# A mixture-of-experts step threaded through attention: expert tiles, sorting and fetching moved to other blocks

## The chip, the cores and the metric

The kernel runs on one core of a Trainium2 chip. The metric is the device time of one execution in microseconds. TensorE is called PE, VectorE DVE, ScalarE ACT, GpSimd POOL and SyncE SP, as in the profile.

## The reference

```python
xn = _layernorm(x)                                   # x is (1, 2048, 128)
# attention: 16 heads of 64, no mask
q, k, v = (xn @ W for W in (Wq, Wk, Wv))
attn = softmax(einsum('bqhd,bkhd->bhqk', q, k) * SCALE)
att = einsum('bhqk,bkhd->bqhd', attn, v).reshape(b, s, H * DH) @ Wo + bo
# experts: each token goes to one of 8, by the largest router logit
expert = argmax(softmax(xn @ router_w.T))
h = square(relu(xn @ expert_fc[expert]))             # 128 -> 512
ffn = h @ expert_proj[expert].T                      # 512 -> 128
return x + att + ffn
```

## The kernel before

The attention is cut into 32 blocks: 8 pairs of heads by 4 column blocks of 512 queries. Block n works on pair n // 4 and queries n % 4. A block has 16 steps kt, one for each 128 keys. In each step PE makes the scores of both heads (two matmuls each, lines 969 and 973, into the banks SB), ACT turns them into exponentials (line 529, five buffers per head and a sixth for the last step), and PE makes for the next block the scores whose row maxima are needed there (line 985, banks MB, three of them), which DVE reduces (line 677). Every fourth step PE multiplies the last four steps' exponentials with V (times_v, line 997, 3.6 us). The exponentials are added up over the steps for the denominators: for head 1 always by POOL (line 430), for head 0 in turns by POOL (steps given by on_pool) and by DVE (add_own, line 693, at steps 0, 4, 8, 12, up to four of them in a row).

Around this, each block has small jobs at fixed steps, all of which pass through the one spare bank XB, whose users wait for one another: the denominators (step 4), the inversion by DVE in two halves (steps 4 and 8, line 809), the normalisation by POOL (step 9, line 436), the projection by Wo (step 11, line 1043), summed into Y by DVE (line 816), the turned row maxima (step 12), Q for the block three ahead (step 7), and K or V of the next pair (steps 1 and 9; blocks with n % 4 of 0 or 1 make K, the others V; the last four blocks make neither). SP issues the copies of Q and K, the row maxima, and all loads from its one queue, in program order.

The experts work on sorted tokens. In the prologue PE makes the router's logits, choose() takes each token's expert. In block 0, rank() (from line 766) computes for each token its slot in a list sorted by expert, padded to tiles of 128, and which expert owns each of the 23 tiles. POOL writes the 16 groups of 128 tokens to their slots in DRAM (sort_tokens, line 454, one indirect DMA each), two per step in the second half of block 0. The tokens come from xn, which lies in the buffer V[1]. In blocks 1 to 23, one tile each, SP loads the tile's tokens and its expert's weights at the block's beginning (load_tile), PE turns the tokens at step 2, multiplies up at step 3 and down at step 6, ACT and POOL do the parts between, and SP stores the result. In block 28 POOL fetches the results of all tokens, 16 indirect DMAs (fetch_results, line 460), into V[0], and in block 29 DVE adds them to Y in four parts (take_back, line 795).

All engines run their own lists in program order and wait for semaphores, so an engine that waits holds up everything behind it in its list.

## Time and profile before

| | us |
|---|---|
| median of 3 runs (1451.12 to 1452.48) | 1451.62 |
| the profiled execution | 1452.27 |
| its span | 1450.5 |
| PE busy | 1398.2 (96%) |
| DVE busy | 1162.4 (80%) |
| ACT busy | 737.3 (51%) |
| POOL busy | 1075.5 (74%) |

The profile is one execution; 1.8 us lie outside its span. Blocks are cut below at the start of the copy in line 566, which ends each block's sum with V. A busy PE can still run at half clock, so the granted clock is read beside the busy time.

### The profile page before, as it was taken

The numbers are of one execution on the slowest core, as the hardware profiler recorded it, in microseconds if no ns is written. First come the engines' busy times: TensorE is split into PE (matmuls) and PEld (weight loads), VectorE is DVE, ScalarE is ACT, GpSimd is POOL, SyncE is SP. The second block draws the span as 40 slices with busy tenths as digits, with TensorE's granted clock in tenths as the row PEclk, the third lists the DMA queues.
The fourth block names the chain that finished last, engine by engine and source line by source line (L and its number), as shares of the span: only waits on it lengthen the run. The fifth ranks groups of instructions, "written<-read, shape, count | busy, mean of one in ns | idle before, by whom it ended". The sixth has DMA issues, their size and how long they took to land.

```text
span 1450.5 us, 20040 instructions
## 1 busy us (share of the span) xinstructions
PE 1398.2 (96%) x6427; PEld 862.4 (59%) x6427; DVE 1162.4 (80%) x1550; ACT 737.3 (51%) x1314; POOL 1075.5 (74%) x851
## 2 busy tenths in 40 slices
PE   5876999999999999999999999999999999999997
PEld 3544665665666665666665666666656565655553
DVE  7875878877888877888878887887788888889865
ACT  4333554555554554554555555555555455544553
POOL 8266777777777777777776777777777777788887
PEclk9898999999999999999999999999999999999998
DMA  3422211321122311132112221122111220001000
GB/s 80 108 62 61 58 41 41 82 63 45 28 62 69 86 25 35 44 90 64 40 25 60 68 64 41 41 68 66 43 41 24 66 68 23 23 24 28 1 15 15
DMA packets 64967, 72.09 MB, mean 50 GB/s; under 512 B 8928, under 2 KB 38112, under 8 KB 64864
## 3 DMA queue, kind: packets, MB, share of 16 engines
q1 hardware_dynamic: 63840, 68.72, 19.2%
q0 software_dynamic: 1024, 2.10, 0.5%
q8 instruction: 52, 0.85, 0.3%
q14 instruction: 51, 0.42, 0.1%
HBM read 17.83 MB, written 5.11 MB: 16 GB/s over the span
## 4 chain that ended last, share of the span: by engine, by line
PE 89%; DVE 5%; POOL 3%; issue 2%; ACT 1%; DMA 1%; POOLq 0%; SPq 0%; DVEq 0%; ACTq 0%
PE OB L997 29%; PE SB L969 17%; PE MB L985 15%; PE SB L973 15%; PE XB L1034 2%; PE XB L1043 2%; PE XB L1025 2%; DVE mx L677 2%; PE XB L952 1%; PE XB L959 1%; POOL acc L430 1%; DVE acc L693 1%; POOL sorted_x L454 1%; PE XB L1004 1%; PE XB L1006 1%
## 5 line engine op out<-in xcount | busy, mean ns | idle before, releaser
L430 POOL TENSOR_TENSOR acc<-acc,ex 128x512 f32<-128x512 f32 x662 | 872.1, 1338 | 171.1 <-ACT ex L529 143.1
L529 ACT ACTIVATE ex<-SB 128x512 f32<-128x512 f32 x1024 | 608.6, 599 | 476.9 <-PE SB L973 420.1
L677 DVE TENSOR_REDUCE mx<-MB 128x1 f32<-128x512 f32 x1024 | 682.5, 686 | 200.5 <-PE MB L985 198.4
L997 PE MATMUL OB<-ex,V 128*64 128x512 f32 x2048 | 467.0, 598 | 0.0
L969 PE MATMUL SB<-Q,K 128*128 128x512 f32 x1024 | 427.9, 418 | 0.0
L985 PE MATMUL MB<-K,Q 128*128 128x512 f32 x1024 | 407.4, 402 | 15.3 <-DVE mx L677 13.9
L973 PE MATMUL SB<-Q,K 128*128 128x512 f32 x1024 | 402.5, 393 | 1.6 <-DMA Q<-mrow 1.6
L693 DVE TENSOR_TENSOR acc<-acc,ex 128x512 f32<-128x512 f32 x234 | 290.3, 1241 | 38.9 <-POOL acc L430 26.7
L997 PEld LDWEIGHTS OB<-ex,V 128*64 128x64 f32 x2048 | 138.6, 137 | 271.3 <-issue 239.7
L969 PEld LDWEIGHTS SB<-Q,K 128*128 128x128 f32 x1024 | 194.2, 190 | 139.3 <-issue 103.0
L985 PEld LDWEIGHTS MB<-K,Q 128*128 128x128 f32 x1024 | 194.9, 191 | 66.9 <-DVE mx L677 23.9
L973 PEld LDWEIGHTS SB<-Q,K 128*128 128x128 f32 x1024 | 194.0, 189 | 33.1 <-DMA Q<-mrow 2.1
L430 POOL TENSOR_TENSOR acc<-ex 128x512 f32<-128x512 f32 x63 | 79.6, 1284 | 96.3 <-ACT ex L529 96.2
L809 DVE RECIPROCAL rd<-rd 128x256 f32<-128x256 f32 x62 | 108.0, 1742 | 0.0
L436 POOL TENSOR_TENSOR osb<-osb,rd 128x512 f32<-128x512 f32 x31 | 39.7, 1281 | 85.3 <-DVE rd L809 85.3
L566 ACT ACTIVATE osb<-OB 128x512 f32<-128x512 f32 x32 | 19.1, 598 | 101.0 <-PE OB L997 101.0
L1034 PE MATMUL XB<-acc,ones 128*64 128x512 f32 x128 | 34.5, 617 | 2.7 <-POOL acc L430 2.7
L1025 PEld LDWEIGHTS XB<-wraw,xT 128*128 128x128 f32 x256 | 34.4, 195 | 2.5
L799 DVE SCALAR_TENSOR_TENSOR qlo<-XB,qhi 128x512 fp32r<-128x512 f32 x31 | 21.4, 692 | 17.8 <-ACT qhi L540 17.6
L1043 PEld LDWEIGHTS XB<-wo,osb 128*128 128x128 f32 x248 | 32.5, 191 | 3.8 <-issue 1.4
L1025 PE MATMUL XB<-wraw,xT 128*128 128x128 f32 x256 | 34.5, 279 | 0.0
L1043 PE MATMUL XB<-wo,osb 128*128 128x128 f32 x248 | 32.7, 275 | 1.0 <-issue 1.0
(126 smaller groups left out, 566.8 us busy)
## 6 DMA issues: line engine op xcount, KB each, us to landing
Q<-qhi SPq DMA_DIRECT2D x124, 128.0 KB, 2.3
K<-khi SPq DMA_DIRECT2D x112, 128.0 KB, 2.3
Q<-qlo SPq DMA_DIRECT2D x64, 128.0 KB, 2.3
K<-klo SPq DMA_DIRECT2D x56, 128.0 KB, 2.3
w<-fc SPq DMA_DIRECT2D x23, 256.0 KB, 2.7
w<-projT SPq DMA_DIRECT2D x23, 256.0 KB, 3.1
sorted_x<-res SPq DMA_DIRECT2D x1, 1472.0 KB, 7.0
tok<-sorted_x SPq DMA_DIRECT2D x23, 64.0 KB, 1.7
```

Source lines behind the costliest of these rows:

```text
L430: pool.tensor_tensor(a[:, :], src[:, :], EX[h][ex_slot(kt)][:, :], ALU.add).then_inc(done, 1)
L529: act.activation(EX[h][ex_slot(kt)][:, :], SB[in_ring(2 * kt + h)][:, :], ACT.Exp).then_inc(a_e[h], 1)
L677: dve.tensor_reduce(mx[:, m % 2, u:u + 1], MB[in_ring(i)][:, :], AX.X, ALU.max).then_inc(v_m, 1)
L693: dve.tensor_tensor(a[:, :], src[:, :], EX[0][ex_slot(kt)][:, :], ALU.add).then_inc(sums[0][n % 2], 1)
L809: dve.reciprocal(rd[:, cols], rd[:, cols]).then_inc(v_rd, 1)
L969: pe.matmul(tile[:, :], K1[par][h][:, keys], Q1[k][h][:, :], start=True, stop=False)
L973: pe.matmul(tile[:, :], K2[par][h][:, keys], Q2[k][h][:, :], start=False, stop=True).then_inc(t_s, 1)
L985: pe.matmul(MB[in_ring(i)][:, :], Q1[k][h][:, q * P:(q + 1) * P], K1[par][h][:, c * QB:(c + 1) * QB], start=True, stop=True).then_inc(t_m, 1)
L997: mm = pe.matmul(OB[own[h], :], V[(n // JB) % 2][:, k, own[h]], EX[h][ex_slot(k)][:, :], start=(k == 0), stop=(k == NT - 1))
L1025: mm = pe.matmul(XB[:, k * P:(k + 1) * P], xT[:, tok], wraw[pair % 2][:, 2, :], start=True, stop=True)
L1034: mm = pe.matmul(XB[own[h], :], ones[:, 0:DH], acc[h][n % 2][:, :], start=True, stop=True)
L1043: mm = pe.matmul(XB[:, q * P:(q + 1) * P], on[:, q * P:(q + 1) * P], wo_s[pair % 2][:, :], start=True, stop=True)
```

## The change

Tiles are worked on in blocks 3 to 25 instead of 1 to 23. SP stores a tile's result and loads the next tile in the middle of a block, behind the K copies and ahead of the Q copies; the first tile is loaded at the end of block 2. The ranking's matmuls move from step 5 to step 3 of block 0, and rank() is cut in three, for steps 4, 8 and 12; the owners of the tiles are found in block 1, step 12. The 16 sorts go one by one into steps 13 to 15 of block 0 and 1 to 13 of block 1. ACT therefore waits for them before it overwrites V[1] in block 2. The fetches go into blocks 28 and 29 (five each) and 30 (six), and their target is the buffer xT. take_back is moved to steps 1, 2, 3 and 5 of block 31, and the sums into Y that come after it wait for it. The division of head 0's additions changes: in block 0 POOL takes all steps with kt % 4 of 1 or 2, in block 1 only those with 1, and block 28, where DVE had all of them, is like the others.

```diff
--- before.py
+++ after.py
@@ -92,8 +92,13 @@
 AT_INV, AT_ON = (4, 8), 9
 AT_TOK, AT_UP, AT_DOWN = 2, 3, 6
 TILES = NT + E - 1
-AT_Q2, AT_RANK = 2, 5
-BACK = (4, 5, 6, 7)
+TILE0 = 3
+AT_Q2, AT_RANK = 2, 3
+AT_PLACE, AT_OWN = (4, 8, 12), (1, 12)
+SORT = [(0, kt) for kt in range(13, NT)] + [(1, kt) for kt in range(1, 14)]
+FETCH = [(n, kt) for n in (NB - 4, NB - 3) for kt in (2, 5, 8, 11, 14)] + [(NB - 2, kt) for kt in range(2, 13, 2)]
+BACK = (1, 2, 3, 5)
+assert FETCH[0][0] >= TILE0 + TILES and len(SORT) == len(FETCH) == NT
 
 
 def layer(nc, x, wq, wk, wv, wo, bo, router_wT, fc, projT, out):
@@ -130,6 +135,7 @@
         acc = [[sb(f"acc{h}{k}", [P, QB]) for k in range(2)] for h in range(2)]
 
         xn = V[1]
+        back = xT[:, :].rearrange("p (t d) -> p t d", d=D)
         halves, mean_var = sb("halves", [P, NT, 6]), sb("mean_var", [P, NT, 2])
         std, rstd = sb("std", [P, NT]), sb("rstd", [P, NT])
         bob, eps = sb("bob", [P, D]), sb("eps", [P, 1])
@@ -214,9 +220,7 @@
 
         def on_pool(n, kt):
 
-            if n.i is None and n.off == NB - JB:
-                return False
-            return kt % BATCH == 1 or (kt % BATCH == 2 and (n.i is not None or n.off > 0 or kt > NT - BATCH))
+            return kt % BATCH == 1 or (kt % BATCH == 2 and n.off != 1)
 
         def ex_slot(kt):
 
@@ -284,7 +288,7 @@
 
         def has_tile(n):
 
-            return n.i is not None or 0 < n.off <= TILES
+            return TILE0 <= n.off < TILE0 + TILES
 
         with nc.Block() as block:
             @block.sync
@@ -382,25 +386,27 @@
 
                 def one(n):
                     pair = n // JB
-                    if has_tile(n):
-                        sp.wait_ge(d_sort, 16 * NT)
-                        sp.wait_ge(v_own, 1)
-                        load_tile(n - 1)
                     if n % JB == 1:
                         if before(n, NB - 2 * JB):
                             load_w(pair + 2)
                     spread = kv_jobs(n) if before(n, NB - JB) and n % JB < 2 else [None, None]
                     if spread[0]:
                         spread_k(*spread[0][1:])
+                    if has_tile(n):
+                        store_tile(n - TILE0)
+                    if has_tile(n + 1) and n.off >= TILE0:
+                        load_tile(n + 1 - TILE0)
                     for kt in range(NT):
                         for m in q_jobs(n, kt):
                             spread_q(m)
                     if spread[1]:
                         spread_k(*spread[1][1:])
-                    if has_tile(n):
-                        store_tile(n - 1)
                     if n % JB == 1 and before(n, NB - JB):
                         load_wo(pair + 1)
+                    if n.off == TILE0 - 1:
+                        sp.wait_ge(d_sort, 16 * NT)
+                        sp.wait_ge(v_own, 1)
+                        load_tile(Lin(0))
                     if before(n, NB - 1):
                         place_max(n + 1)
 
@@ -408,6 +414,7 @@
                     ov = out.rearrange("o (t p) d -> p (o t) d", p=P)
                     for j in range(JB - 1):
                         sp.wait_ge(v_y, NB - JB + j + 1)
+                        sp.wait_ge(v_back, j + 1)
                         sp.dma_start(chunk(ov, j), chunk(Y, j)).then_inc(d_out, 16)
                     for q in range(TB):
                         k = NT - TB + q
@@ -455,9 +462,9 @@
 
                 def fetch_results(ks):
                     pool.wait_ge(d_res, 16 * (TILES + 1))
-                    pool.wait_ge(t_pv, NT * (NB - JB))
+                    pool.wait_ge(t_v, NB)
                     for k in ks:
-                        pool.indirect_dma_start(V[0][:, k, :], None, sorted_y, indexed(k)).then_inc(d_back, 16)
+                        pool.indirect_dma_start(back[:, k, :], None, sorted_y, indexed(k)).then_inc(d_back, 16)
 
                 def first():
                     pool.memset(res[:, :], 0.0).then_inc(g_i, 1)
@@ -506,14 +513,14 @@
                         if kt == AT_ON and not (n.i is None and n.off == 0):
                             normalise(n - 1)
                         if kt == AT_UP + 1 and has_tile(n):
-                            square(n - 1)
+                            square(n - TILE0)
                         if on_pool(n, kt):
                             add(n, kt, 0)
                         add(n, kt, 1)
-                        if kt >= 8 and n.i is None and n.off == 0:
-                            sort_tokens((2 * kt - NT, 2 * kt - NT + 1))
-                        if n.i is None and n.off == NB - JB:
-                            fetch_results((kt,) if kt > 1 else (0, 1))
+                        if (n.off, kt) in SORT:
+                            sort_tokens((SORT.index((n.off, kt)),))
+                        if (n.off, kt) in FETCH:
+                            fetch_results((FETCH.index((n.off, kt)),))
 
                 schedule(pool, first, one, lambda: None)
 
@@ -549,6 +556,8 @@
                         act.activation(khi[:, :], XB[:, :], ACT.Copy).then_inc(a_k, 1)
                     else:
                         wait(act, t_v, pair.times(JB, c + 1))
+                        if pair.off == 1:
+                            wait(act, d_sort, 16 * NT)
                         wait(act, t_pv, pair.times(NT * JB, 1 - NT * JB))
                         act.activation(V[pair % 2][:, c * TB:(c + 1) * TB, :].rearrange("p t d -> p (t d)"), XB[:, :],
                                        ACT.Copy).then_inc(a_v, 1)
@@ -650,11 +659,11 @@
                             kv(*kv_jobs(n)[AT_KV.index(kt)])
                         if has_tile(n):
                             if kt == AT_TOK:
-                                copy_tokens(n - 1)
+                                copy_tokens(n - TILE0)
                             if kt == AT_UP:
-                                rectify(n - 1)
+                                rectify(n - TILE0)
                             if kt == AT_DOWN:
-                                take_result(n - 1)
+                                take_result(n - TILE0)
                         if kt == 0 and n % JB == 0 and before(n, NB - JB):
                             split_w(n // JB + 1)
                         if kt == 0 and not (n.i is None and n.off == 0):
@@ -762,7 +771,15 @@
                     step(dve.tensor_reduce(top[:, :], pick[:, :, :].rearrange("p e t -> p t e"), AX.X, ALU.max))
                     dve.tensor_tensor(mask[:, :, :], pick[:, :, :], under(top[:, :], E), ALU.is_equal).then_inc(v_mask, 1)
 
-                def rank():
+                def rank(part):
+                    if part == 0:
+                        count_tokens()
+                    elif part == 1:
+                        first_tiles()
+                    else:
+                        find_slots()
+
+                def count_tokens():
 
                     earlier = XB[:, 0:NT * E].rearrange("p (e t) -> p e t", e=E)
                     dve.wait_ge(t_rk, 1)
@@ -774,6 +791,8 @@
                     dve.wait_ge(v_mask, 2)
                     step(dve.tensor_tensor(place[:, :, :], place[:, :, :], cum[:, :, :], ALU.add))
                     step(dve.tensor_tensor(place[:, :, :], place[:, :, :], total[:, :, :], ALU.subtract))
+
+                def first_tiles():
                     step(dve.tensor_tensor(total[:, :, :], cum[:, :, NT - 1:NT].to_broadcast([P, E, NT]),
                                            under(tokens_in[:, :], E), ALU.is_gt))
                     step(dve.tensor_reduce(tiles_of[:, :], total[:, :, :], AX.X, ALU.add))
@@ -781,18 +800,23 @@
                     step(dve.tensor_tensor(first_tile[:, :], end[:, :], tiles_of[:, :], ALU.subtract))
                     step(dve.scalar_tensor_tensor(out=place[:, :, :], in0=over(first_tile[:, :], NT), scalar=float(P),
                                                   in1=place[:, :, :], op0=ALU.mult, op1=ALU.add))
+
+                def find_slots():
+
                     step(dve.tensor_tensor(place[:, :, :], place[:, :, :], mask[:, :, :], ALU.mult))
                     step(dve.tensor_reduce(top[:, :], place[:, :, :].rearrange("p e t -> p t e"), AX.X, ALU.add))
                     dve.tensor_copy(slot[:, :], top[:, :]).then_inc(v_slot, 1)
 
+                def find_owners():
+
                     step(dve.tensor_tensor(past[:, :, :], over(tile_no[:, :], E), under(end[:, :], TILES), ALU.is_ge))
                     step(dve.tensor_reduce(owner[:, :], past[:, :, :], AX.X, ALU.add))
                     dve.tensor_scalar(owner_i[:, :], owner[:, :], float(E - 1), None, ALU.min).then_inc(v_own, 1)
 
                 def take_back(j):
                     dve.wait_ge(d_back, 16 * NT)
-                    dve.wait_ge(v_y, NB - JB)
-                    dve.tensor_tensor(chunk(Y, j), chunk(Y, j), chunk(V[0], j), ALU.add).then_inc(v_back, 1)
+                    dve.wait_ge(v_y, NB - 2)
+                    dve.tensor_tensor(chunk(Y, j), chunk(Y, j), chunk(back, j), ALU.add).then_inc(v_back, 1)
 
                 def low_q(m):
                     wait(dve, a_q, m.times(1, 1))
@@ -810,7 +834,7 @@
 
                 def sum_up(n):
                     wait(dve, t_wo, n.times(1, 1))
-                    if n.i is None and n.off == NB - JB:
+                    if n.off == NB - 2:
                         dve.wait_ge(v_back, JB)
                     y = Y[:, (n % JB) * TB:(n % JB + 1) * TB, :].rearrange("p t d -> p (t d)")
                     dve.tensor_tensor(y, XB[:, :], y, ALU.add).then_inc(v_y, 1)
@@ -864,9 +888,11 @@
                             add_own(n, kt)
                         if kt in AT_INV and not start:
                             invert(n - 1, AT_INV.index(kt))
-                        if start and kt == AT_RANK:
-                            rank()
-                        if n.i is None and n.off == NB - JB + 1 and kt in BACK:
+                        if start and kt in AT_PLACE:
+                            rank(AT_PLACE.index(kt))
+                        if (n.off, kt) == AT_OWN:
+                            find_owners()
+                        if n.off == NB - 1 and kt in BACK:
                             take_back(BACK.index(kt))
                         if kt == AT_WO:
                             if start:
@@ -889,6 +915,7 @@
 
                     def sum_tile(q):
                         y = Y[:, NT - TB + q, :]
+                        dve.wait_ge(v_back, JB)
                         dve.wait_ge(t_wo, NB + q)
                         dve.tensor_tensor(y, LAST[q][:, 0:P], y, ALU.add).then_inc(v_y, 1)
 
@@ -1090,11 +1117,11 @@
                             ranks()
                         if has_tile(n):
                             if kt == AT_TOK:
-                                turn_tokens(n - 1)
+                                turn_tokens(n - TILE0)
                             if kt == AT_UP:
-                                expert_up(n - 1)
+                                expert_up(n - TILE0)
                             if kt == AT_DOWN:
-                                expert_down(n - 1)
+                                expert_down(n - TILE0)
                         if kt in AT_KV and before(n, NB - JB):
                             make_kv(*kv_jobs(n)[AT_KV.index(kt)])
                         for m in q_jobs(n, kt):
```

## Rows read from the trace of the kernel before

**Rows 1.** The page, the chain that ended last, by engine.

```profile
PE 89%; DVE 5%; POOL 3%; issue 2%; ACT 1%; DMA 1%; POOLq 0%; SPq 0%; DVEq 0%; ACTq 0%
```

**Rows 2.** Busy time by block: core:, us, PE, PEld, DVE, ACT, POOL busy, PEclk, DMA share, GB/s.

```profile
109.42:166.66 57.24, 44.91 (x200) 27.83 (x201) 36.56 (x47) 23.01 (x42) 40.38 (x33) 0.88 0.29 75
166.66:210.05 43.39, 43.39 (x210) 27.42 (x211) 33.79 (x44) 22.89 (x42) 32.74 (x25) 1.00 0.13 34
253.43:296.67 43.24, 43.19 (x200) 26.68 (x201) 35.32 (x46) 23.03 (x42) 32.24 (x25) 1.00 0.31 75
1119.56:1160.49 40.93, 40.93 (x183) 24.89 (x184) 34.58 (x46) 21.96 (x38) 31.63 (x24) 1.00 0.25 59
1242.84:1284.23 41.39, 41.39 (x193) 25.56 (x194) 34.18 (x44) 21.96 (x38) 31.77 (x24) 1.00 0.09 20
1284.23:1328.82 44.59, 41.53 (x177) 24.65 (x178) 41.46 (x51) 20.99 (x36) 37.65 (x32) 0.96 0.15 40
1328.82:1369.72 40.90, 39.55 (x174) 23.06 (x175) 37.12 (x49) 20.49 (x36) 33.58 (x25) 1.00 0.01 3
1369.72:1406.54 36.82, 36.82 (x164) 20.95 (x165) 28.32 (x33) 19.61 (x36) 31.77 (x24) 1.00 0.05 15
```

**Rows 3.** PE in order of time, blocks 0, 1, 28: start, us, engine, line, what.

```profile
79.40 0.80 PE L985 MATMUL MB<-K,Q 128*128 128x512 f32 x1 [5.67 <-DVE mx L677]
...
104.33 0.50 PE L973 MATMUL SB<-Q,K 128*128 128x512 f32 x1 [1.63 <-DMA Q<-mrow]
...
125.63 0.45 PE L946 MATMUL XB<-ident,tok 128*128 128x128 f32 x1 [11.25 <-DMA w<-projT]
...
1310.31 0.79 PE L985 MATMUL MB<-K,Q 128*128 128x512 f32 x1 [2.48 <-DVE mx L677]
```

**Rows 4.** Busy time in the stretch after the first stall, columns as in rows 2.

```profile
79.40:87.14 7.74, 7.74 (x23) 3.43 (x23) 5.88 (x8) 1.19 (x2) 3.62 (x3) 0.67 0.02 8
```

**Rows 5.** DVE in order of time, blocks 0 and 28.

```profile
71.40 0.28 DVE L769 COPY w<-XB 128x128 f32<-128x128 f32 x1
...
75.01 0.29 DVE L777 TENSOR_TENSOR w<-w,tokens_in 128x128 f32<-128x128 f32 x1
...
77.01 0.29 DVE L784 TENSOR_TENSOR w<-w 128x128 f32<-128x128 f32 x1
...
78.67 2.47 DVE L677 TENSOR_REDUCE mx<-MB 128x1 f32<-128x512 f32 x4
...
1302.63 5.42 DVE L693 TENSOR_TENSOR acc<-acc,ex 128x512 f32<-128x512 f32 x4
```

**Rows 6.** ACT and SP's queue in order of time, block 5.

```profile
312.63 0.28 ACT L616 ACTIVATE res<-XB 128x128 f32<-128x128 f32 x1 [0.52 <-PE XB L959]
...
316.06 1.10 SPq L305 DMA_DIRECT2D Q<-qhi  x2
...
330.78 0.33 SPq L349 DMA_DIRECT2D tok<-sorted_x  x1
```

**Rows 7.** Groups of instructions by line, and one projection in the chain of waits.

```profile
L430 POOL TENSOR_TENSOR acc<-acc,ex 128x512 f32<-128x512 f32 x662 | 872.1, 1338 | 171.1 <-ACT ex L529 143.1 <-POOL acc L430 0.5
...
L460 POOL DMA_INDIRECT V<-sorted_y,slot x16 | 17.4, 1088 | 2.7 <-POOL acc L430 1.6 <-issue 0.6
...
324.60 0.89 PE XB L1043 x8
```

**Rows 8.** POOL in order of time, blocks 30 and 31.

```profile
1371.04 2.53 POOL L430 TENSOR_TENSOR acc<-ex 128x512 f32<-128x512 f32 x2 [2.51 <-ACT ex L529]
...
1407.86 2.54 POOL L430 TENSOR_TENSOR acc<-ex 128x512 f32<-128x512 f32 x2 [0.95 <-ACT ex L529]
...
1425.31 1.27 POOL L436 TENSOR_TENSOR osb<-osb,rd 128x512 f32<-128x512 f32 x1 [0.59 <-DVE rd L809]
1426.54 14.96 POOL L430 TENSOR_TENSOR acc<-acc,ex 128x512 f32<-128x512 f32 x11
```

**Rows 9.** One line: ns min/median/max of each, first and last start.

```profile
L795 DVE TENSOR_TENSOR Y<-Y,V x4: 620/828/1799, 1339.0 to 1345.0; 128x512 f32<-128x512 f32 x4
```

## The prediction

> **What bounds the kernel now.** I read the chain of waits first, since it names the engine that sets the end: TensorE (PE) holds 89% of it [rows 1]. Then I cut the span into the 32 blocks, at the copy of the finished attention sum (line 566) that each block makes once, and read length, busy time and granted clock of each [rows 2]. What the reader is to see there: in the middle PE is busy for the whole of a block at clock 1.00, so there only PE's own work counts; blocks 1, 28 and 29 (and 0, by its own rows) are longer than that work, and blocks 1 and 28 also have a clock below 1.00, that is, a part of them at 1.2 GHz instead of 2.4. The length of a block is set by which jobs it has, and three rows give the clean ones: 40.93 us for a block that makes K and has no expert tile, 41.39 for one that makes V and has none, 43.24 and 43.39 for the same two with a tile [rows 2]. So a tile costs PE 43.24 - 40.93 = 2.31 us beside K jobs and 43.39 - 41.39 = 2.00 beside V jobs. Then the stalls by PE's own timeline [rows 3], and what VectorE (DVE) and GpSimd (POOL) did in and near them [rows 5, 8].
>
> **Block 0: the ranking in three parts.** Now DVE does all of rank() at once, from 71.40 to 78.67, 7.3 us without one row maximum [rows 5]; PE runs out of free banks for the maxima and stands still 5.67 us [rows 3]. Afterwards its clock is low: from 79.40 to 87.14 it was granted 0.67, so (1 - 0.67) x 7.74 = 2.55 us more are lost [rows 4]. Together 8.2 us. The change leaves count_tokens in one piece at step 4, 71.40 to 75.01 = 3.6 us, first_tiles (75.01 to 77.01, 2.0 us) at step 8, find_slots at step 12 and find_owners in block 1; the last two share the 1.66 us from 77.01 to 78.67 [rows 5]. What burst PE tolerates is seen in block 28: four additions and an inversion, 5.42 + 1.66 us from 1302.63, made PE wait 2.48 us [rows 3, 5], so about 7.1 - 2.5 = 4.6 us are hidden behind the product with V. New bursts: step 4, two additions (step 2 now goes to POOL) at 5.42/4 each make 2.7, with 3.6 it is 6.3, which would cost 1.7; additions that meet no POOL addition are shorter and the counting shared its time with POOL's, so I take 1.0 (bounds 0 and 1.7). Step 8: 2.7 + 2.0 = 4.7, nothing. Step 12: 2.7 + 0.8, nothing. A stall of 1.63 at 104.33 kept the clock up [rows 2, 3], so I count no clock loss for 1.0. The matmuls for the ranking come two steps earlier and only trade places with others. The 1.63 us at 104.33, a wait for the row maxima's DMA behind the Q and K copies in SP's queue [rows 3], stays: the order of that queue in block 0 is the same. Gain 8.2 - 1.0 = 7.2 us (6.0 to 8.2).
>
> **Block 1: no tile, but 13 of the sorts.** Now PE waits 11.25 us for the first tile's weights, which are loaded only after 16 sorts have landed [rows 3]; with the slow clock behind it and the tile itself the block takes 57.24 instead of 40.93 us, 16.3 more [rows 2]. All of it goes if nothing new is late. What could be: POOL. Its work there is 19 additions of 1.34 (line 430: 872.1 us over 662), one normalisation of 1.3 and 13 sorts, each priced as a fetch, 1.09 [rows 7], and about 0.2 us between instructions: 25.5 + 1.3 + 16.8 = 44 us against 41. From the block's mark POOL starts at 1.3 (1371.04 in block 30, whose mark is 1369.72), and up to step 8 it has 10 additions and 8 sorts: 1.3 + 13.4 + 10.3 = 25.0, so the normalisation ends at 26.3. PE's projection, which waits for it, comes 324.60 - 296.67 = 27.9 after the mark in block 5, 25.6 without that block's tile [rows 2, 7, 8]: 0.7 too early. DVE has 11 additions instead of 7; its bursts are three additions and an inversion, 3 x 1.36 + 1.7 = 5.8, against 4.6 to 5.3 (a K job lies between): 0.5. I take 0.5 for DVE and 0.4 for POOL, bounds 0 and 5, the upper one being what block 28 with its 16 fetches lost, 44.59 - 39.6 (below). The gain is 16.3 - 0.9 = 15.4 us (11.3 to 16.3). POOL leaves the block about 2 us behind; block 2 has idle time for that.
>
> **Block 2 and ScalarE's new wait.** Without its tile block 2 goes from 43.39 to 41.39: gain 2.0. ScalarE now waits for all sorts before it overwrites V[1] at step 1 of block 2, and behind that wait stand its exponentials. The last sort is queued at step 13 of block 1; with POOL 2 us late it lands about when the V job's product is done. I take 0, bounds 0 and 2.
>
> **The middle.** Tiles are 23 before and after, in blocks 3 to 25 instead of 1 to 23. In the middle nothing changes for PE; blocks 24 and 25 gain a tile each beside K jobs: 2 x 2.31 = 4.6 us of cost. SP now stores tile n-3 and loads the next inside block n. In block 5 the result is there at 312.63 + 0.28 and the Q copies are issued from 316.06 [rows 6]; the store and the load need about 0.4 + 2.3 us of issue (from the read of the owner ahead of 330.78 to the last weight DMA), so they fit into a gap in SP's queue that is 3.1 us long. The store leaves the place ahead of the row maxima. Effect 0.
>
> **Blocks 28 and 29.** A clean block 28 is 41.39 less two V jobs. Those are 8 matmuls each, which take 0.89 us of the chain, as in the projection [rows 7]: 41.39 - 1.8 = 39.6; block 29 has no Q job either (0.7 us): 38.9. Now they take 44.59 and 40.90, DVE having all 15 additions of head 0 in block 28 (four of them in the burst above) and take_back in block 29 [rows 2, 5]. After, DVE has 7 additions in each and POOL 8 more plus 5 fetches. POOL is busy 31.6 of a clean 40.93 [rows 2], that is 9.3 idle; a fetch costs 1.09 [rows 7] and about 0.2 around it, 1.29, five of them 6.5. The block is 1.3 and 2.0 us shorter, which leaves 8.0 and 7.3: enough. Gain 5.0 + 2.0 = 7.0 (4 to 7).
>
> **Blocks 30 and 31: here something is given back.** Block 30 gets six fetches, 6 x 1.29 = 7.7 us, onto POOL. It is idle there 36.82 - 31.77 = 5.05 us, but 2.51 of that lies ahead of step 1, before the first fetch [rows 2, 8]. From 1407.86 to the last addition (the run of 11 that ends at 1441.5) POOL works with one gap of 0.59: in block 31 POOL sets the end [rows 8]. What can be filled is 2.5 and the 0.95 ahead of 1407.86, so 7.7 - 3.5 = 4.2 us reach the end. take_back moves from block 29 to block 31, four DVE additions of 0.62 to 1.80 us with both operands in SBUF [rows 9]. DVE is mostly idle there, but POOL's additions are stretched by such instructions (mean 1.34, against 1.27 for each of the two at 1371.04) [rows 7, 8]; I take 0.3 for each, 1.2 in all (0 to 2.4). The Trainium skill, page "SBUF — State Buffer", section "Who interferes with whom", states that a DVE instruction with two SBUF inputs and a GpSimd one that reads SBUF hold the port in turn, the second waiting until the first is finished. By it up to 4 x 0.69 = 2.8 us could go to POOL if DVE always came first; the 1.80 row shows DVE waiting instead, so the trace bears out the rule with DVE mostly second. Cost of the tail 4.2 + 1.2 = 5.4 (0 to 8).
>
> **Sum.** -7.2 - 15.4 - 2.0 + 4.6 - 7.0 + 5.4 = -21.6 us. The profiled execution took 1452.27 us (span 1450.5), 0.65 above the median; it becomes 1430.7, and against the median 1430.0.
>
> **The rivals.** (a) The tail costs nothing: POOL's lag is hidden as exponentials and additions have five buffers per head. Against it speaks the unbroken run of POOL in block 31. Then 1430.0 - 5.4 = 1424.6. (b) Block 1 becomes what block 28 is now: DVE and POOL both over PE's 41 us, a stall above 2.4 us and the clock down again. For it: 44 us of POOL work by my own count. It costs 4.1 more than I took, and ScalarE's wait up to 1: 1435. (c) The tail is dearer: normalisation and exponentials, late behind POOL, stop PE long enough that its clock falls: 2.6 us on top of the upper bound of 8: 1435. Together with (b) 1440. (d) The split of the ranking doesn't do its work, as count_tokens with its additions is still a burst that drops the clock: the 7.2 us counted are not gained, 1437. (e) Slower: SP. Its store waits for the tile's result in mid-block, ahead of the Q copies, in each of 23 blocks. If the result is late or the weights' DMA hold up the Q halves and the maxima behind them, PE waits in each block. From 21.6/23 = 0.94 us per block the gain is gone; at 1.2 us it is 1430 + 27.6 = 1458. Against it: the Q copies are not needed before the next-but-one block, and the gap of 3.1 us.
>
> **How the numbers follow.** Forecast case 0.55, 1426 to 1434; (a) 0.12, (b) 0.15, (c) 0.08, (d) 0.06, (e) 0.03, leaving 0.01 for less than 0.2%, which is about what a measurement of this kernel can tell from no change (2.9 us). Range 1424 to 1438, which takes in (a), (b) and most of (c) and (d). Faster 0.96, same 0.01, slower 0.03.
>
> **What would show it.** In the profile after: no idle stretch on PE above about 1.7 us in blocks 0 and 1, and block 1 about 42 us long (if 45 with a clock under 1, it is (b)); block 24 near 43.2; blocks 28 and 29 at 39.6 and 38.9 with clock 1.00; POOL without a gap from the middle of block 30 on and block 31 near 37 us (if near 32.5, it is (a)). A wait on ScalarE for the sorts in block 2, or idle PE in every tile block, would prove steps above wrong. The forecast falls most easily with the tail, whose price rests on POOL alone, and with block 1.

## The result, and the profile after

The changed kernel takes 1433.87 us (median, 1433.47 to 1434.51); the kernel before took 1451.73 beside it. The ratio is 0.9877, with a 95% interval of 0.9860 to 0.9894, so it is faster by 17.9 us. The forecast was 1430.0 with a range of 1424 to 1438: right in sign and within the range, 3.9 us too low.

The profiled execution has a span of 1431.7 us against 1450.5. Its blocks, cut at the same copy as before (columns as in rows 2; the first row starts at about PE's first scores of block 0, 56.53, the others at the copy's start):

```profile
56.56:103.17 46.61, 44.52 (x185) 25.97 (x184) 38.63 (x62) 22.70 (x41) 32.67 (x26) 0.98 0.32 76
103.17:147.97 44.80, 42.13 (x183) 24.58 (x184) 42.17 (x53) 21.93 (x38) 40.18 (x34) 1.00 0.29 75
147.97:189.36 41.39, 41.39 (x193) 25.56 (x194) 35.00 (x45) 21.94 (x39) 32.01 (x25) 1.00 0.14 35
...
1141.97:1185.20 43.23, 43.17 (x200) 26.69 (x201) 35.31 (x46) 22.99 (x42) 32.23 (x25) 1.00 0.25 59
1267.97:1307.54 39.57, 39.57 (x177) 23.77 (x178) 34.30 (x44) 20.97 (x36) 35.95 (x29) 1.00 0.11 27
1307.54:1346.80 39.26, 39.19 (x174) 23.14 (x175) 34.70 (x43) 20.48 (x35) 36.48 (x30) 1.00 0.04 10
1346.80:1383.63 36.83, 36.83 (x164) 20.95 (x165) 24.32 (x32) 19.60 (x36) 35.24 (x29) 1.00 0.05 13
1383.63:1420.98 37.35, 32.73 (x136) 16.13 (x136) 23.34 (x15) 16.42 (x32) 35.43 (x27) 0.95 0.08 21
```

Against rows 2 the reader sees block 1 at 44.80 instead of 57.24, block 2 at 41.39 instead of 43.39, block 25 at 43.23 (a tile is in it now), blocks 28 and 29 at 39.57 and 39.26 instead of 44.59 and 40.90, and block 30 unchanged. Block 31 is 37.35 now: here time is given back. In the kernel before it was

```profile
1406.54:1439.03 32.49, 31.41 (x136) 14.92 (x136) 14.11 (x10) 16.42 (x32) 29.98 (x24) 1.00 0.03 9
```

so it now also has a part at 1.2 GHz (0.95 instead of 1.00). Where PE still waits stands in its own order of time:

```profile
98.10 0.50 PE L1000 MATMUL SB<-Q,K 128*128 128x512 f32 x1 [1.63 <-DMA Q<-mrow]
...
117.53 0.50 PE L1012 MATMUL MB<-K,Q 128*128 128x512 f32 x1 [0.89 <-DVE mx L686]
...
129.18 0.50 PE L1012 MATMUL MB<-K,Q 128*128 128x512 f32 x1 [0.76 <-DVE mx L686]
...
1407.33 2.05 PE L1070 MATMUL XB<-wo,osb 128*128 128x128 f32 x8 [4.57 <-issue]
```

The 5.67 and 11.25 us of rows 3 are gone. There are short waits for DVE in block 1 (a third of its kind stands at 141.1) and one of 4.57 us for the normalisation in block 31. At the same place the kernel before waited 1.03 us:

```profile
1426.68 1.13 PE L1043 MATMUL XB<-wo,osb 128*128 128x128 f32 x8 [1.03 <-issue]
```

DVE and POOL around the new waits:

```profile
110.26 5.01 DVE L702 TENSOR_TENSOR acc<-acc,ex 128x512 f32<-128x512 f32 x3
115.19 1.74 DVE L833 RECIPROCAL rd<-rd 128x256 f32<-128x256 f32 x1
...
138.86 1.55 DVE L814 TENSOR_SCALAR owner_i<-owner 128x23 int32<-128x23 f32 x1
```

```profile
137.79 1.25 POOL L461 DMA_INDIRECT sorted_x<-V,slot  x1 [0.17 <-POOL acc L437]
139.07 1.29 POOL L437 TENSOR_TENSOR acc<-acc,ex 128x512 f32<-128x512 f32 x1
...
1380.22 6.69 POOL L437 TENSOR_TENSOR acc<-acc,ex 128x512 f32<-128x512 f32 x5
1386.86 3.41 POOL L437 TENSOR_TENSOR acc<-ex 128x512 f32<-128x512 f32 x2
1390.23 15.11 POOL L437 TENSOR_TENSOR acc<-acc,ex 128x512 f32<-128x512 f32 x10
1405.96 1.26 POOL L443 TENSOR_TENSOR osb<-osb,rd 128x512 f32<-128x512 f32 x1 [0.62 <-DVE rd L833]
```

Block 1's three additions at step 4 need 5.01 us, 1.67 each in the mean; one by one they take 2.27, 0.69 and 1.84 us, and the short one is the one that runs beside a sort of POOL and not beside an addition. The last step of find_owners, an instruction of 0.18 us in the kernel before (at 78.58), takes 1.55. POOL runs without a gap from block 30 into block 31: its first addition there starts 3.2 us after the block's mark, where it started 1.3 us after it before (rows 8).

### The profile page after: what moved, and what is told of

The parts are those of the page before. It is cut to its first block, busy times and chain, and to the rows that moved or that the text cites. A ratio compares the mean times of both kernels' runs of the same rounds, so it can differ in the third digit from the quotient of the medians.

```text
span 1431.7 us, 20036 instructions
## 1 busy us (share of the span) xinstructions
PE 1394.3 (97%) x6427; PEld 859.2 (60%) x6427; DVE 1163.4 (81%) x1543; ACT 736.6 (51%) x1314; POOL 1083.7 (76%) x858
## 4 chain that ended last, share of the span: by engine, by line
PE 87%; DVE 7%; issue 2%; POOL 2%; ACT 1%; SPq 1%; DMA 0%; POOLq 0%; DVEq 0%
PE OB L1024 28%; PE SB L996 16%; PE MB L1012 15%; PE SB L1000 14%; DVE mx L686 3%; PE XB L1061 2%; PE XB L1052 2%; PE XB L1070 2%; POOL acc L437 2%; PE XB L986 1%; PE XB L979 1%; DVE acc L702 1%; PE XB L1031 1%; PE XB L1033 1%; PE XB L1032 1%
```

## The experiments

All are variants of the changed kernel, unless it is said otherwise. Ratios are to the kernel before on the same chip; the changed kernel had 0.9877, and 0.9876 when it was run again. Since the intervals are about 0.17% wide to each side, blocks of the traces decide between theories, and the times only confirm.

**1. One part undone: the ranking in one piece.**

```diff
-AT_Q2, AT_RANK = 2, 3
+AT_Q2, AT_RANK = 2, 5
-                        if start and kt in AT_PLACE:
-                            rank(AT_PLACE.index(kt))
-                        if (n.off, kt) == AT_OWN:
-                            find_owners()
+                        if start and kt == AT_RANK:
+                            for part in range(3):
+                                rank(part)
                             find_owners()
```

> The changed kernel, but the ranking undivided at step 5 of block 0, as it was before (the owners with it). Theory of the burst (the three parts are worth what PE no longer waits): a stall of about 5.7 us on PE and 2.5 us of slow clock come back in block 0, while block 1 loses the 2.2 us that find_owners takes on DVE there: 1433.9 + 8 - 1 = about 1441 us. Rival (the split is worth little, since the two additions that went to POOL already shorten the burst): 1434 to 1437 us.

Measured: ratio 0.9913 (0.9896 to 0.9929), 1441.19 us. PE and the two blocks:

```profile
80.82 0.80 PE L1012 MATMUL MB<-K,Q 128*128 128x512 f32 x1 [7.00 <-DVE mx L686]
```

```profile
56.56:110.17 53.61, 44.85 (x184) 26.50 (x183) 40.85 (x64) 22.72 (x41) 32.14 (x26) 0.93 0.28 66
110.17:153.74 43.57, 41.80 (x183) 24.66 (x184) 39.46 (x50) 21.96 (x39) 39.10 (x33) 1.00 0.30 77
```

Block 0 ends 7.0 us later, with a stall of 7.00 and a fallen clock, and block 1 is 1.2 shorter, which prices find_owners in block 1 at 1.2 us. Block 31 is 38.87 us, 1.5 longer than in the changed kernel, with the same wait of PE (4.58) but a lower clock (0.91 against 0.95), in a block that this edit doesn't touch; without it the expected 1441 would have been some 1.5 us too high. The burst theory holds; the rival is out.

**2. One part alone: in the kernel before, each tile one block later.**

```diff
-            return n.i is not None or 0 < n.off <= TILES
+            return n.i is not None or 1 < n.off <= TILES + 1
-                        load_tile(n - 1)
+                        load_tile(n - 2)
+                        if pair.off == 1:
+                            wait(act, d_sort, 16 * NT)
```

(and n - 2 for n - 1 at each of the tile's other steps)

> The kernel before with one part of the change alone: each tile one block later (blocks 2 to 24), and ScalarE's wait for the sorts before it overwrites V[1]. Theory of the tile wait: the 11.25 us wait in block 1 and the 1.6 us of slow clock behind it vanish, block 1 becomes about 42.5 us (40.9 and a stall from POOL's 16 sorts), a tile leaves it and comes back in block 24: 1451.7 - 12.5 = about 1439 us. Rival (the wait comes back elsewhere, as POOL is still 9 us behind at the start of block 1 and DVE waits for it): 1443 us or more.

Measured: ratio 0.9953 (0.9936 to 0.9970), 1446.56 us, about 7 less than the kernel before and not 12.5. Its block 1, with DVE and PE:

```profile
109.71:158.22 48.51, 43.44 (x183) 25.80 (x184) 36.37 (x47) 21.96 (x38) 39.86 (x32) 0.96 0.28 71
```

```profile
123.24 3.37 DVE L695 TENSOR_TENSOR acc<-acc,ex 128x512 f32<-128x512 f32 x2 [4.34 <-POOL acc L430]
```

```profile
128.87 0.64 PE L987 MATMUL MB<-K,Q 128*128 128x512 f32 x1 [3.86 <-DVE mx L679]
```

With the tile out of the way another wait comes up: POOL is behind by its 16 sorts, DVE waits 4.34 us for it, PE 3.86 for DVE, and the clock falls. The rival holds. In the kernel before, the wait for the tile had covered this one, so moving the tile without spreading the sorts brings only 57.24 - 48.51 = 8.7 us in block 1.

**3. Block 1's additions back on POOL.**

```diff
-            return kt % BATCH == 1 or (kt % BATCH == 2 and n.off != 1)
+            return kt % BATCH == 1 or kt % BATCH == 2
```

> The changed kernel, but in block 1 POOL takes the additions of steps 2, 6, 10 and 14 as in other blocks, beside its 13 sorts. Theory DVE (the 3.9 us that block 1 is over 40.9 come from DVE's 11 additions, each stretched by POOL's): DVE's stalls go, but 4 x 1.33 us more on POOL, which has no idle time there, appear as a late normalisation and late additions: block 1 not shorter, 1434 to 1437 us. Theory POOL-free (POOL has slack in block 1, only DVE counts): about 1431 us.

Measured: ratio 0.9893 (0.9877 to 0.9910), 1438.36 us; block 1 is 48.38 us:

```profile
131.78 1.13 PE L1070 MATMUL XB<-wo,osb 128*128 128x128 f32 x8 [1.88 <-issue]
...
143.71 0.50 PE L1012 MATMUL MB<-K,Q 128*128 128x512 f32 x1 [3.00 <-DVE mx L686]
```

The two waits at DVE's first two bursts are gone, but PE waits 1.88 us for the late normalisation and 3.00 later. So POOL has no room for these additions beside 13 sorts, even less than I expected: the block is 3.6 us longer. Not all of it is room: just ahead of the wait of 3.00, find_owners takes 4.0 us on DVE (139.09 to 143.05) instead of 2.3. And block 31 is 38.92 us here, 1.6 more than in the changed kernel, with a lower clock (0.91).

**4. The old tail on the new front.** Fetches, additions and take_back at the steps of the kernel before; the fetches' target stays xT (not shown: the waits that go with it):

```diff
-FETCH = [(n, kt) for n in (NB - 4, NB - 3) for kt in (2, 5, 8, 11, 14)] + [(NB - 2, kt) for kt in range(2, 13, 2)]
+FETCH = [(NB - 4, max(k, 1)) for k in range(NT)]
-            return kt % BATCH == 1 or (kt % BATCH == 2 and n.off != 1)
+            return n.off != NB - JB and (kt % BATCH == 1 or (kt % BATCH == 2 and n.off != 1))
-BACK = (1, 2, 3, 5)
+BACK = (4, 5, 6, 7)
-                        if n.off == NB - 1 and kt in BACK:
+                        if n.off == NB - 3 and kt in BACK:
```

> The changed kernel with the old tail: all 16 fetches in block 28, DVE has all additions of head 0 there, take_back in block 29. Theory (the new tail gains 6.7 us in blocks 28 and 29 and gives 4.1 back after block 30, net 2.6): 1433.9 + 2.6 = 1436.5 us. Rival (the tail's parts are separate, the loss in block 31 comes from elsewhere): block 31 stays at 37 us and the time is about 1440 us.

Measured: ratio 0.9882 (0.9865 to 0.9898), 1436.14 us. Its blocks 28, 29 and 31:

```profile
1268.10:1312.93 44.83, 41.73 (x177) 24.82 (x178) 41.52 (x51) 20.98 (x36) 37.64 (x32) 0.96 0.15 40
1312.93:1352.69 39.76, 39.53 (x174) 23.06 (x175) 36.00 (x49) 20.50 (x35) 34.16 (x25) 1.00 0.01 3
1389.51:1422.00 32.49, 31.40 (x136) 14.93 (x136) 14.11 (x10) 16.43 (x33) 29.98 (x24) 1.00 0.03 9
```

Block 31 is back at 32.49, so its loss comes from the new tail. The new tail wins 5.3 and 0.5 us in blocks 28 and 29 and loses 4.9 in block 31 (block 29 is 39.76 even with the old tail and not 40.90, so 1.1 us of what block 29 gained isn't shown to be the new tail's); with the ends of the kernels the spans differ by 2.0 us (1433.7 against 1431.7). By the ratios, 0.9882 and 0.9877, the difference is within the measurement's uncertainty. Nearly the whole gain of the changed kernel is in its front.

**5. The changed kernel again**, to stand beside the next three.

> The changed kernel itself, to stand beside the next three on the same chip. About 1434 to 1436 us; block 1 at 44.8 us and block 31 at 37.4, or at 38.9 where PE's clock falls after its 5 us wait there.

Measured: 0.9876 (0.9859 to 0.9893), 1434.62 us; block 1 at 44.84, block 31 at 37.63. The clock falls in block 31 here too, as it did in the first execution (0.95 in both).

**6. Sorts spread over three blocks.**

```diff
-SORT = [(0, kt) for kt in range(13, NT)] + [(1, kt) for kt in range(1, 14)]
+SORT = [(0, kt) for kt in range(13, NT)] + [(1, kt) for kt in (2, 4, 7, 10, 12, 14)] + \
+    [(2, kt) for kt in (1, 2, 4, 5, 7, 8, 10)]
-            return kt % BATCH == 1 or (kt % BATCH == 2 and n.off != 1)
+            return kt % BATCH == 1 or kt % BATCH == 2
```

(with a second semaphore for the late sorts)

> The changed kernel with the 16 sorts spread as 3, 6 and 7 over blocks 0, 1 and 2 (instead of 3 and 13), and block 1's additions divided as in other blocks. Theory of the overfull block (block 1 is 3.9 us over a clean 40.9 as POOL has 13 sorts on top of a full block, and DVE 4 additions for it): with 6 sorts x 1.25 us in the 9 us that POOL is idle, block 1 falls to about 41.2 and block 2 stays at 41.4 us: 3.5 us less. Rival (block 1's excess is the port between DVE's and POOL's additions, whatever the sorts do, or the start from block 0): at most 1 us less.

Measured: ratio 0.9919 (0.9903 to 0.9936), 1441.03 us: slower by 6 us instead of faster by 3.5. The waits at DVE's additions are gone, and two others stand in block 1 and at the end of block 2:

```profile
141.82 0.50 PE L1015 MATMUL MB<-K,Q 128*128 128x512 f32 x1 [4.62 <-DVE mx L689]
...
189.09 0.50 PE L1003 MATMUL SB<-Q,K 128*128 128x512 f32 x1 [1.98 <-DMA Q<-mrow]
```

Behind the first, DVE and POOL:

```profile
135.99 5.19 DVE L817 TENSOR_SCALAR owner_i<-owner 128x23 int32<-128x23 f32 x1
```

```profile
136.20 4.93 POOL L438 TENSOR_TENSOR acc<-acc,ex 128x512 f32<-128x512 f32 x4
141.30 0.98 POOL L462 DMA_INDIRECT sorted_x<-V,slot  x1 [0.17 <-POOL acc L438]
```

An instruction on 23 numbers per partition takes 5.19 us: it starts while POOL works on a sort and ends only when POOL's next four additions are through. Behind the second wait is SP, whose wait for the last sort (step 10 of block 2) holds up the row maxima: they are issued at 186.27, and PE, which is there at 187.1, waits for them until 189.09. Block 1 is 47.64 us and block 2 is 45.48. Neither outcome that I had written down came, and neither had this; whether the spread itself is right is left to number 10.

**7. Four additions of block 31 to DVE.**

```diff
-            return kt % BATCH == 1 or (kt % BATCH == 2 and n.off != 1)
+            return kt % BATCH == 1 or (kt % BATCH == 2 and n.off not in (1, NB - 1))
```

> The changed kernel, but in block 31 DVE takes the additions of steps 2, 6, 10 and 14 from POOL. Theory of the tail (POOL's unbroken run from block 30 on sets the end; DVE is idle in block 31): POOL loses 4 x 1.35 us, block 31 goes from 37.4 to about 33 us: 4 us less, more where the clock no longer falls. Rival (the end is set by the fetches' landing or by take_back on DVE): no change, or slower as DVE has 4 x 1.67 us more.

Measured: ratio 0.9864 (0.9847 to 0.9880), 1433.37 us; block 31 at 37.56 us, as in the changed kernel (37.63); the 1.2 us by which the span is shorter (1431.7 against 1432.9 in number 5) lie behind the block's end. So POOL alone isn't the limit there. In its place:

```profile
1391.55 5.17 DVE L702 TENSOR_TENSOR acc<-acc,ex 128x512 f32<-128x512 f32 x3
1396.64 1.74 DVE L833 RECIPROCAL rd<-rd 128x256 f32<-128x256 f32 x1
1398.30 1.61 DVE L819 TENSOR_TENSOR Y<-Y,xT 128x512 f32<-128x512 f32 x1
1399.83 5.14 DVE L702 TENSOR_TENSOR acc<-acc,ex 128x512 f32<-128x512 f32 x3
1404.90 1.74 DVE L833 RECIPROCAL rd<-rd 128x256 f32<-128x256 f32 x1
```

DVE works without a gap up to the inversion, with its additions at 1.7 us in the mean beside POOL's, and POOL waits 2.29 us for it. The work ahead of the normalisation was moved from one full engine to the other.

**8. Fetches earlier.** 3, 6, 5 and 2 in blocks 27 to 30:

```diff
-FETCH = [(n, kt) for n in (NB - 4, NB - 3) for kt in (2, 5, 8, 11, 14)] + [(NB - 2, kt) for kt in range(2, 13, 2)]
+FETCH = [(NB - 5, kt) for kt in (11, 13, 15)] + [(NB - 4, kt) for kt in (2, 4, 6, 9, 11, 14)] + \
+        [(NB - 3, kt) for kt in (2, 5, 8, 11, 14)] + [(NB - 2, kt) for kt in (3, 7)]
```

> The changed kernel with the 16 fetches at 3, 6, 5 and 2 in blocks 27 to 30 instead of 5, 5 and 6 in blocks 28 to 30. Theory of the tail (what POOL cannot do in block 30 is added at the end, 4.2 us by the prediction's sum): blocks 28 and 29 stay, block 31 goes from 37.4 to about 34 us (the rest is take_back's 1.6 us): 3.5 us less. Rival (only take_back costs): unchanged.

Measured: ratio 0.9856 (0.9840 to 0.9872), 1432.12 us. Block 31 is 34.88 us, 2.8 less, and block 28 is 40.77, 1.2 more: two of DVE's additions (at 1287.23) take 3.81 us there instead of 2.36, and PE waits 0.88 us for the row maxima behind them. In block 31 POOL's first addition starts 1.3 us after the mark again, and PE waits 1.88 us instead of 4.61, while the clock is as low as before (0.95). The theory of the tail holds in mechanism and nearly in size for block 31.

**9. Without take_back.** Its four additions are left out, so the output lacks the experts' part.

```diff
-                    dve.tensor_tensor(chunk(Y, j), chunk(Y, j), chunk(back, j), ALU.add).then_inc(v_back, 1)
+                    dve.sem_inc(v_back, 1)
```

> The changed kernel without the four additions of take_back: the experts' results are left out of the output, everything else stays, the semaphore is raised by hand. It prices take_back in block 31. Theory of the port (each of the four stretches POOL's additions, which set the pace, by 0.4 us, as 3.41 against 2.54 for two of them and 15.11 against 14.37 for ten show): block 31 falls from 37.4 to about 35.8 us, 1.6 less. Rival (take_back costs by holding DVE's additions back): more than 3 us less. Rival (nothing, DVE is idle there): under 0.5 us.

Measured: ratio 0.9852 (0.9836 to 0.9868), 1431.49 us; block 31 at 35.83 us against 37.35 and 37.63: 1.5 to 1.8 us.

```profile
1382.99:1418.82 35.83, 32.97 (x136) 15.97 (x136) 16.98 (x11) 16.53 (x33) 33.69 (x27) 0.95 0.08 22
```

```profile
1404.93 1.69 PE L1070 MATMUL XB<-wo,osb 128*128 128x128 f32 x8 [2.81 <-issue]
```

PE's wait is 1.76 us shorter than the 4.57. POOL's twelve additions ahead of the normalisation, 3.41 + 15.11 us in the changed kernel, take 2.51 + 14.24 here, 1.77 less: take_back costs what it stretches them by. What is left over the 32.49 of the kernel before is 3.3 us: 1.8 of wait (2.81 against 1.03) and, by difference, some 1.5 of slow clock.

**10. The sorts at 3, 8 and 5, and find_owners in block 2.**

```diff
-AT_PLACE, AT_OWN = (4, 8, 12), (1, 12)
+AT_PLACE, AT_OWN = (4, 8, 12), (2, 1)
...
+SORT = [(0, kt) for kt in range(13, NT)] + [(1, kt) for kt in (2, 3, 5, 7, 8, 10, 12, 14)] + \
+    [(2, kt) for kt in (1, 3, 4, 6, 7)]
-            return kt % BATCH == 1 or (kt % BATCH == 2 and n.off != 1)
+            return kt % BATCH == 1 or kt % BATCH == 2
```

(not shown: the old SORT and the second semaphore, as in number 6)

> The changed kernel with the sorts at 3, 8 and 5 over blocks 0 to 2 (the last at step 7, before SP waits for them), block 1's additions divided as elsewhere, and find_owners in block 2, step 1. Theory (what failed in sort_spread were two things of its own: an owner instruction that found POOL in a run of four additions and waited 5 us, and a last sort that held up SP's row maxima in block 2; the spread itself is right): block 1 falls from 44.8 to about 41.3 us, block 2 stays at 41.4: 3.4 us less than the changed kernel. Rival (block 1 is long whatever the sorts do): block 1 above 43 us.

Measured: ratio 0.9884 (0.9867 to 0.9900), 1436.31 us. Blocks 1 and 2:

```profile
103.73:144.70 40.97, 40.97 (x183) 24.92 (x184) 35.52 (x46) 21.95 (x39) 37.56 (x32) 1.00 0.30 73
144.70:193.01 48.31, 44.10 (x193) 26.67 (x194) 39.77 (x48) 21.94 (x38) 38.78 (x31) 0.93 0.14 38
```

```profile
146.87 2.83 DVE L815 TENSOR_TENSOR up<-tile_no,end 128x184 f32<-128x184 f32 x1
149.74 0.34 DVE L816 TENSOR_REDUCE owner<-up 128x23 f32<-128x184 f32 x1
150.12 3.07 DVE L817 TENSOR_SCALAR owner_i<-owner 128x23 int32<-128x23 f32 x1
```

Block 1 is a clean block, 3.8 us shorter than in the changed kernel: its excess was the crowding by sorts, additions and owners, as the theory said. The three were taken out together; only the owners' share, 1.2 us, is known by itself (experiment 1). But find_owners met POOL's runs again, now in block 2: 6.3 us for three instructions, PE waits 4.21 us, the clock falls, and 6.9 us are lost.

**11. An even tail.** Fetches at 3, 5, 5 and 3 in blocks 27 to 30, take_back at steps 5, 7, 9 and 10, and:

```diff
+            if (n.off, kt) in ((NB - 2, 10), (NB - 2, 13), (NB - 2, 14), (NB - 1, 13), (NB - 1, 14)):
+                return False
```

> The changed kernel with the fetches at 3, 5, 5 and 3 in blocks 27 to 30, take_back at steps 5, 7, 9 and 10 of block 31, and five additions of head 0 on DVE instead of POOL: steps 10, 13 and 14 of block 30 and 13 and 14 of block 31. Theory (in block 31 neither POOL nor DVE alone is the limit ahead of step 9 but both, as they share the chain of head 0 and stretch each other; work must leave POOL in block 30 and not come to DVE before the inversion): block 31 falls from 37.4 to about 33 us, PE's wait of 4.6 us for the normalisation to under 1.5: 4 us less. Rival (fetches and additions cannot be moved without making DVE the limit, as in b31_dve): block 31 stays above 36 us.

Measured: ratio 0.9844 (0.9828 to 0.9861), 1429.91 us. Block 31 falls to 33.70, with blocks 28 and 29 as in the changed kernel and the clock at 1.00. PE still waits 2.23 us for the normalisation, where I expected under 1.5; of the 3.65 us that the block is shorter, 2.3 are wait and, by difference, 1.3 are clock:

```profile
1383.45:1417.15 33.70, 31.41 (x136) 14.94 (x136) 23.63 (x16) 16.42 (x33) 30.38 (x22) 1.00 0.08 24
```

**12. Numbers 10 and 11 together, and in block 0 the row maxima ahead of the second K copies.** (The edits of both, and in SP's list place_max moved ahead of spread_k for block 0; not shown.)

> sort_owner and tail_even together, and in block 0 SP issues the row maxima ahead of the second K copies. If the parts add up: 3.4 us and 4 us less, and the 1.6 us that PE waits for the row maxima at the start of block 1: 9 us less than the changed kernel, about 1426 us where that one takes 1435.

Measured: ratio 0.9848 (0.9832 to 0.9865), 1430.93 us, no better than number 11. The tail's gain is there (block 31 at 33.73), the wait of 1.6 us at the start of block 1 is gone (block 0 ends at 101.44, block 1 is 41.35 us), and block 2, with find_owners, takes it all back at 47.36. Number 11 has the lowest ratio of the complete versions, about 4.7 us below the changed kernel; numbers 12 and 8 lie within its interval. The front of number 12 with find_owners left in a place where POOL has no run was not tried.

## Why the prediction was right, and where it was off

- **Ranking in parts: right.** Block 0 ends 6.3 us earlier (109.42 to 103.17), although PE's first scores of block 0 came 0.5 us later than before, so the block itself is 6.8 us shorter; 7.2 was forecast. count_tokens cost no stall at all where 1.0 was taken (its instructions ran at their short durations), so two small errors met: no cost where 1.0 was taken, and some 1.4 us less to be had than the 8.2 that the sum counted as lost. Where these went isn't shown; the first product with V already comes 1.1 us later after the first scores than before, of which about 0.4 are the ranking's matmuls. Experiment 1 gives 7.0 for the undoing.
- **Block 1: mechanism right, term mis-sized.** 12.4 us were gained, not 15.4. Taken was an excess of 0.9 over the clean 40.93; measured is 3.9. The step that failed is the price of a DVE addition: 1.36 us, the mean of a burst of four in block 28, against means of 1.67 and 1.45 here. Both are mixtures: one by one the four took 1.90, 0.69, 1.82 and 0.69, two beside a POOL addition and two beside a fetch, and the three of block 1 took 2.27, 0.69 and 1.84, so here two of three were the long kind. That makes bursts of 6.8 and 6.1 us with the inversion instead of 5.8, and waits of PE of 0.89 and 0.76. And find_owners has no term in the sum of block 1 at all, where it cost 1.2. The three waits make 2.6 of the 3.9; the other 1.2 or so lies in PE's busy time (42.13 against 40.93) at clock 1.00, and its cause is open. The normalisation, on the edge by the sum, did not stop PE, but had no room left: experiment 3.
- **What I had not seen at all:** that in the kernel before the wait for the tile hid a second one. It didn't falsify the sum, as the change moved the sorts as well, but the tile's move alone is worth 8.7 us in that block and not the 16.3 that the sum puts on it (experiment 2).
- **ScalarE's wait, the middle, SP: right.** ScalarE copies V in block 2 with 0.52 us of wait for PE and none for the sorts; blocks with a tile are 43.2 and 43.4 as before; SP's store and load fit between the copies. Rival (e) is out in its form, but its mechanism is real: a last sort at step 10 of block 2 makes SP late for the row maxima (experiment 6).
- **Blocks 28 and 29: 6.7 us gained, 7.0 forecast.** Experiment 4 shows 5.8 of them to be the new tail's.
- **The tail: 4.9 us lost in block 31 (5.4 forecast), of which 0.75 comes back behind it.** The total is near, partly by luck. take_back was forecast at 1.2 and measured at 1.5 to 1.8. The other term, 4.2 us of POOL's work that reaches the end, was too large: POOL comes to block 31 only 1.9 us late (3.2 us after the mark instead of 1.3), and without take_back PE's wait is 1.8 us over the old one. What fills the gap is a cost that the sum put at nothing and only rival (c) named: PE's clock falls around the wait (0.95), and of the 4.9 us 1.3 are left for it by difference, when the longer wait (4.57 against 1.03) is taken off. Rival (c) was right in this and wrong in its price, since it set the fall on top of a loss of 8. And "POOL sets the end" was only half of it: ahead of the normalisation DVE is nearly as full, and the two stretch each other (experiment 7). What helps is to take work off POOL in block 30 (experiments 8 and 11).
- **Added up** by the marks: 6.3 + 12.4 + 2.0 - 4.5 + 6.7 - 4.9 + 0.7 = 18.7 us, the difference of the spans being 18.8. Forecast 21.6; 3.0 of the 2.9 missing are block 1's, the other terms cancel.

## What to carry to other kernels

When the longest wait in a stretch is taken away, ask who else was late behind it: here POOL's backlog was hidden under the wait for a tile (11.25 us), and came up as waits of 4.34 us on DVE and 3.86 on PE. A burst's price is read from a row in which the neighbouring engine does what it will do after the change, and one instruction at a time, since an addition took 0.69 us beside a sort or a fetch and 1.6 to 2.3 beside an addition of POOL, and a mean mixes them. Work spread thin over blocks is free only where both engines of a shared chain have room; in the last block nothing comes after to absorb a backlog, so it should be empty before that.

## What the runs showed of the hardware

A small DVE instruction can wait for a whole run of POOL additions, not only for one: the last instruction of find_owners, 0.18 us in the kernel before, took 1.55 us in the changed kernel (one addition), 3.07 in variant 10 (two of a run of three) and 5.19 in variant 6 (a run of four, 4.93 us). Each time it started in the last 0.2 to 0.5 us of a sort and ended with the additions behind that sort. The Trainium skill, page "SBUF — State Buffer", section "Who interferes with whom", says of a DVE instruction in a two-port mode and GpSimd that whoever issues first has the shared pair for its whole instruction and the other is blocked. No run shows whether this instruction is in such a mode. By the starts in the trace it came ahead of the additions that held it (138.86 against 139.07, 135.99 against 136.20); even if it counts as second behind the sort, the 5.19 doesn't fit the rule, as four additions that started later went ahead of it. DVE's own additions, which take turns with POOL's in one chain, were never held that long: the longest in any of these traces took 2.46 us (variant 4), the longest of the changed kernel 2.27.

From the start of block 0 to the end of block 31, every wait of PE of 2.53 us and more in these traces (2.53, 2.81, 3.00, 3.86, 4.21 and longer) had 1.2 GHz behind it or already within it. Shorter ones went either way: with 2.48 us the clock fell (block 28 of the kernel before), with 2.49 in the same block it stayed at 2.4 GHz (variant 2); it fell with 1.98 (variant 6) and 1.88 us (variant 8), and stayed with 2.26 (variant 12), 2.23 (variant 11), another 1.88 (variant 3) and everything up to 1.63. In block 31 of the changed kernel the same wait of 4.6 us went with a granted clock of 0.95 and a block of 37.35 us in one execution and 37.63 in another, and with 0.91 in the variants 1, 3, 6 and 10, where the block took 38.87, 38.92, 38.46 and 37.95, so up to 1.5 us of the kernel's time hang on how the fall of the clock meets the work.
